# Another order of routing, projections and stack copies in the turns of a fused attention and mixture-of-experts kernel

## The chip, the core and the metric

One core of a Trainium2 chip runs the whole layer as one program. The metric is the device time of one execution in microseconds. Three runs of the kernel before gave 364.13, 364.21 and 365.44 us; the median is 364.21 us.

## What is computed

The input `x` is 4 batches of 512 tokens of width 256. It is normalized per token to `xn`, and the output is `x + attention(xn) + moe(xn)`, all in float32.

```
q = xn @ Wq (16 heads of 16); k = xn @ Wk, v = xn @ Wv (one head shared by all)
q, k = rope(q), rope(k)                      # first 8 of 16 dimensions
scores = q k^T / 4, allowed where 0 <= i - j < 64
attention = softmax(scores) v, heads joined, @ Wo + bo
logits = xn @ router_w; top 4 of logits + router_bias; gates = softmax(logits) of these, normalized to sum 1
routed = sum over the 4 of gate * (silu(xn wg_e) * (xn wu_e)) wd_e      # 64 experts, 256 x 64 x 256
shared = sum over 2 of (silu(xn swg) * (xn swu)) swd                    # hidden 256
```

## The kernel before, in words

The 2048 tokens are 16 tiles of 128. Each engine has a queue of its own, in an order written out by hand; semaphores tie them. In this kernel TensorE is `tensor(pe)`, ScalarE `scalar(act)`, VectorE `vector(dve)`, GpSimd `gpsimd(pool)` and the transfers' queue is `sync(sp)`. In the profile they are PE (its weight loads PEld), ACT, DVE, POOL and SP.

**Stages.** A first stage (to about 28 us) normalizes, transposes x, and makes keys, values and logits. Then comes "turn 0" and a loop of turns `T` = 1 to 15, one per tile of queries (28 to 146 us, turn T beginning where PE starts `maxima(T, 0)`). A tail (146 to 171 us) ends attention and starts the experts. Then 32 groups of four blocks of routed rows (to 277 us) and the shared expert with the sums follow.

**One turn.** Queries come from `project(T)` (L422: a matmul to bank 7 or bank 2; ACT's `copy_q`, L830, takes it to memory) and are rotated by POOL in pairs of tiles (`rotate`, L1517 to L1523: four pieces for a pair; `ROTATED_AT` says in which turn a pair starts, and a piece is done after each scatter of odd index). ACT `cast` (L854) and DVE `leave` (L1098) split them in bf16 parts, PE `stack` (L441) transposes them, ACT `stack` (L863) copies the result. PE `maxima(T, w)` (L463) makes scores by query, DVE `maxima` (L1104) reduces them, DVE `split` (L1113, L1115) cuts the maximum in two. PE `place` (L473) transposes it, DVE `place` (L1122) copies it out, and SP `place` (L1708) sends it by DMA to the rows that next turn's `scores` (L493) use. ACT `scores` (L871) is the exponential; `weigh` (L536) multiplies by values, DVE `output` (L1130) copies, `tokens` (L544), `attention` (L551, L877) and `project_out` (L561) follow. `stack_k` (L447) stands between the two `weigh` of a turn; it shares a bank with `place` and waits until DVE's `place` has read it. `project_out` and `project` share bank 7, each waiting for the reader of the other (`wide_free`).

**Routing.** DVE's `routing()` is a generator: `next(route)` does one piece, and `ROUTE`, `route_at` say how many pieces go before and after `place(T)`. Its seventh and eighth pieces make row numbers `slot_i` (L1231, semaphore `slots`); from then on POOL issues 64 scatters of xn rows (`scatter`, L1533), five in a turn up to T = 8, four later (`SCATTERED_AT`), each behind a wait for a step of PE in that turn. The last pieces make the gates, and from `expert_row` (L591, in turn 13) the experts' offsets `wslice`. SP loads the scattered rows (`load_block`, L1722) in turn 15, when all scatters have landed and the gates are ready.

**Late projections.** Tiles 0 to 6 are projected before turn 1, tile T + 6 in turn T (`late_tile`), between the last scores and `place(T)` on PE; ACT copies the query tile ahead of its second `stack` copy.

## Time and profile before

| what | us |
|---|---|
| median of three runs | 364.21 |
| profiled execution, its own time | 365.55 |
| its span | 364.2 |
| PE busy | 334.7 |
| DVE busy | 252.5 |
| POOL busy | 247.0 |
| ACT busy | 182.0 |

The span begins and ends with the first and last instruction; 1.35 us of the profiled execution lie outside it. Busy shares are means over all stages. For a change in the turns one reads the stretch of the turns: how long each turn takes, which engine was late at its end, and for whom it waited. The starts of the turns 2 to 15 (PE, line 463) are 47.87, 55.93, 63.54, 75.12, 82.95, 90.97, 98.75, 106.42, 113.45, 120.02, 126.49, 133.39, 140.22 and 146.11 us.

### The profile page before, as it was taken

Reading aid. Unit: us, or ns where it says so; the run is one execution under the profiler, and the core shown is the slowest. Engines: PE = TensorE matmul, PEld = TensorE weight load, DVE = VectorE, ACT = ScalarE, POOL = GpSimd, SP = SyncE. Lnnn points to the kernel's source line nnn. Section 1 sums busy time; section 2 is a strip of 40 time slices with the busy share of each in tenths; the row PEclk is TensorE's granted clock in tenths of the full one; section 3 lists DMA queues with packets and bytes.
Section 4 is the critical chain, followed back from the end, with each engine's and each line's share of the span. In section 5 each row is a group of like instructions: output and inputs, shape, how many; then the busy total and the mean of one; then the engine's idle time right before and its main releaser. Section 6 shows DMA issues by size and latency. Waiting matters only on the chain.

```text
span 364.2 us, 8589 instructions
## 1 busy us (share of the span) xinstructions
PE 334.7 (92%) x2711; PEld 248.2 (68%) x2711; DVE 252.5 (69%) x699; ACT 182.0 (50%) x344; POOL 247.0 (68%) x478
## 2 busy tenths in 40 slices
PE   6897879698999999999999999999999999999982
PEld 3795546456665665588999999999975456655572
DVE  4979888878899999555456545444476376667686
ACT  2696686857678787453655655555542111110100
POOL 6487378858778866224665667787884777777773
PEclk9998999989999999999999999999999999999999
DMA  8850245534586546899988855587975334444443
GB/s 247 228 157 1 61 162 158 166 131 158 159 249 199 153 162 173 251 240 265 319 270 264 267 181 169 187 246 254 331 254 161 105 115 130 131 127 121 134 140 115
DMA packets 73036, 66.83 MB, mean 183 GB/s; under 512 B 9053, under 2 KB 68701, under 8 KB 72993
## 3 DMA queue, kind: packets, MB, share of 16 engines
q1 hardware_dynamic: 66433, 49.30, 45.9%
q0 software_dynamic: 6144, 16.79, 14.7%
q8 instruction: 23, 0.38, 0.4%
q10 hardware_dynamic: 416, 0.20, 0.3%
q14 instruction: 20, 0.16, 0.2%
HBM read 36.79 MB, written 29.23 MB: 181 GB/s over the span
## 4 chain that ended last, share of the span: by engine, by line
PE 62%; DVE 12%; issue 8%; ACT 7%; POOL 6%; DMA 4%; SPq 1%; DVEq 0%; ACTq 0%; POOLq 0%
PE bank L669 16%; PE bank L608 15%; PE bank L694 9%; PE bank L628 7%; POOL xs_d L1533 5%; PE bank L643 5%; ACT xall L871 3%; PE bank L561 2%; ACT xall L863 2%; PE bank L536 2%; PE bank L422 2%; DMA spare<-xs_d 2%; DVE xall L1343 1%; DVE xall L1104 1%; DMA wall<-in_x 1%
## 5 line engine op out<-in xcount | busy, mean ns | idle before, releaser
L1533 POOL DMA_INDIRECT xs_d<-spare,slot_i x64 | 63.8, 998 | 30.5 <-issue 9.6
L1625 POOL DMA_INDIRECT wall<-y_d,y_row x64 | 62.8, 981 | 24.3 <-issue 18.9
L669 PE MATMUL bank<-xall,spare 128*128 x508 | 63.8, 278 | 0.0
L1297 DVE TENSOR_TENSOR spare<-bank,spare 64x512 f32<-64x512 f32 (+1 forms) x64 | 44.1, 690 | 28.2 <-ACT spare L912 27.3
L1560 POOL COPY spare<-wall 128x256 f32 x127 | 48.8, 406 | 20.7 <-PE bank L669 11.4
L669 PEld LDWEIGHTS bank<-xall,spare 128*128 128x128 f32 x508 | 59.4, 192 | 2.1
L608 PE MATMUL bank<-xnT,xall 128*128 128x512 f32 x128 | 57.3, 594 | 0.0
L925 ACT ACTIVATE spare<-bank 128x512 f32<-128x512 f32 (+1 forms) x62 | 33.6, 593 | 27.4 <-PE bank L694 21.1
L863 ACT ACTIVATE xall<-bank 98x1024 bf16<-98x1024 bf16 x32 | 32.8, 1025 | 17.6 <-PE bank L441 12.6
L608 PEld LDWEIGHTS bank<-xnT,xall 128*128 128x128 f32 x128 | 24.1, 190 | 25.2 <-issue 24.4
L888 ACT ACTIVATE xall<-bank 128x512 f32<-128x512 f32 x16 | 9.5, 597 | 59.6 <-PE bank L608 59.6
L871 ACT ACTIVATE xall<-bank 128x512 f32<-128x512 f32 x64 | 34.8, 604 | 4.4 <-PE bank L493 3.2
L1343 DVE SCALAR_TENSOR_TENSOR xall<-wall,gate,xall 128x256 f32<-128x256 f32 x64 | 31.1, 487 | 2.3
L912 ACT ACTIVATE spare<-bank 64x512 f32<-64x512 f32 (+1 forms) x32 | 18.8, 588 | 27.5 <-PE bank L669 27.5
L1165 DVE COPY xall<-bank 128x256 f32<-128x256 f32 x32 | 13.6, 424 | 25.2 <-PE bank L643 24.8
L1104 DVE TENSOR_REDUCE xall<-bank 128x4 f32<-128x316 f32 x64 | 28.0, 478 | 3.9 <-PE bank L463 3.5
L628 PEld LDWEIGHTS bank<-xall 128*128 128x128 f32 x128 | 24.2, 190 | 9.3 <-issue 5.3
L628 PE MATMUL bank<-xall 128*128 128x256 f32 x128 | 29.7, 380 | 1.0 <-DVE xall L1328 1.0
L854 ACT ACTIVATE xall<-xall 128x768 bf16<-128x768 f32 (+1 forms) x32 | 23.6, 739 | 11.1 <-POOL xall L1523 9.7
L1311 DVE SCALAR_TENSOR_TENSOR xall<-xall,bank 128x512 f32<-128x512 f32 x16 | 11.0, 687 | 21.4 <-ACT xall L888 21.3
L493 PE MATMUL bank<-xall,wdn 128*128 128x256 bf16 x120 | 20.9, 275 | 3.3 <-DMA xall<-xall 0.9
L441 PE MATMUL bank<-cb,xall 128*98 128x128 bf16 x256 | 20.7, 225 | 3.1 <-ACT xall L863 1.7
(174 smaller groups left out, 614.2 us busy)
## 6 DMA issues: line engine op xcount, KB each, us to landing
y_d<-spare SPq DMA_DIRECT2D x31, 512.0 KB, 3.7
wall<-in_wg SPq DMA_DIRECT2D x16, 256.0 KB, 3.6
wall<-in_wu SPq DMA_DIRECT2D x16, 256.0 KB, 4.2
wdn<-in_wd SPq DMA_DIRECT2D x16, 256.0 KB, 4.4
spare<-xs_d SPq DMA_DIRECT2D x32, 128.0 KB, 3.5
small<-xs_d SPq DMA_DIRECT2D x32, 128.0 KB, 3.4
wall<-in_x SPq DMA_DIRECT2D x4, 512.0 KB, 5.7
base_d<-spare SPq DMA_DIRECT2D x16, 128.0 KB, 3.9
```

The source lines that it names most:

```text
L608: ins = pe.matmul((gate_bank(i), up_bank(i))[half], wsh[:, c, half, ex, f0:f0 + P], xnT[:, c, g * GN:(g + 1) * GN], start=c == 0, stop=c = ...
L628: ins = pe.matmul(shared_bank(T), hs[T // GT % 2][:, k, t * P:(t + 1) * P], wshd[:, k, :], start=k == 0, stop=k == FC - 1)
L669: ins = pe.matmul(up_bank_of(G)[:, j * P:(j + 1) * P], wcur[i % NW][:, c * 2 * F:(c + 1) * 2 * F], x_half[c][:, bass.ds(o, P)], start=c == ...
L694: ins = pe.matmul(o[:, j * P:(j + 1) * P], hT[G % 2][rows64, j * P:(j + 1) * P], down_weights_of(G)[j][rows64, :], start=True, stop=True)
L863: act.activation(qS[0:SROWS + MROWS, T % NQ, :, 8 * i:8 * i + 8, :].rearrange("p u h q -> p h u q"), o[0:SROWS + MROWS].rearrange("p h (u ...
L871: act.activation(probs[n % 2][:, e * 512:(e + 1) * 512], bank[2 + e][:, :], ACT.Exp).then_inc(s["exp"], 1)
L925: act.activation(yb[G % 2][:, 0:n, half * P:(half + 1) * P], o[:, 0:n * P].rearrange("p (j d) -> p j d", d=P), ACT.Copy).then_inc(s["y_out ...
L1297: ins = dve.tensor_tensor(hT[G % 2][half, 0:n], up_bank_of(G)[F:P, 0:n], sg[0:F, 0:n], ALU.mult)
L1343: dve.scalar_tensor_tensor(a, yk[:, T, k, :], gate[:, T, k:k + 1], a, ALU.mult, ALU.add).then_inc(s["sum"], 1)
L1533: pool.indirect_dma_start(out=xs_d, out_offset=bass.IndirectOffsetOnAxis(ap=slot_i[:, T, k:k + 1], axis=0), in_=x_n[b][:, t, :], in_offset ...
L1560: pool.tensor_copy(wcur[i % NW].rearrange("p (c g f) -> p c g f", c=NC, g=2), wall[:, bass.ds(o, WE)].rearrange("p (g c f) -> p c g f", c= ...
L1625: pool.indirect_dma_start(out=yk[:, T, k, :], out_offset=None, in_=of, in_offset=bass.IndirectOffsetOnAxis(ap=y_row[:, T, k:k + 1], axis=0 ...
```

## The change

- **Turn 0**: PE projects tiles 4 to 7 there, not 4 to 6; `project(4)` moves ahead of `stack(1, 0)` and no longer does `kvr_read`; `maxima(1, 0)` of PE and DVE moves from turn 1 into turn 0 (DVE: ahead of the totals piece). POOL rotates tiles 6 and 7 before its first scatter.
- **Turns**: the late tile of turn T is T + 7, so turns 1 to 8 have one; PE does it behind `place(T)`. ACT copies its second stack ahead of the late query tile. DVE does its pieces of routing behind `place(T)` and `near(T + 1)`, ahead of `output(T - 1)`; two pieces in turns 9, 13 and 14, else one.
- **Routing**: the piece of the exponents' maximum comes ahead of the one for the expert of each block; the piece `y_row` stands by itself, later. `expert_row` is in turn 14.
- **POOL**: five scatters in every turn until they run out; the pair of tiles 8 and 9 begins in turn 2, then a pair every second turn to turn 8.

```diff
--- before.py
+++ after.py
@@ -323,11 +323,10 @@
 
     FIRST = 10
 
-    ROUTE = {8: (1, 1), 13: (0, 2)}
-    route_at = lambda T: ROUTE.get(T, (1, 0) if T < 8 else (0, 1))
-    EXPERT_ROW, EXPONENTS, BIAS_AT = 13, 4, 18
-    SCATTERED_AT = lambda T: (0, 1, 2, 3, 4) if T < 9 else (0, 1, 2, 3)
-    ROTATED_AT = {2: 6, 4: 8, 6: 10, 8: 12, 10: 14}
+    route_at = lambda T: 2 if T in (9, 13, 14) else 1
+    EXPERT_ROW, EXPONENTS, BIAS_AT = 14, 4, 18
+    SCATTERED_AT = lambda T: range(5)
+    ROTATED_AT = {2: 8, 4: 10, 6: 12, 8: 14}
     roped_with = lambda T: T + 1 if T < 2 else 2 + T // 2
 
     NORM = ((0,), (1,), (2,), (3,))
@@ -336,9 +335,9 @@
     ready = lambda T: (s["normed_act" if on_act(T) else "normed"], T // TPB * (TPB // 2) + T % (TPB // 2) + 1)
 
 
-    FIRST_LATE = 7
+    FIRST_LATE = 8
     late_tile = lambda T: (FIRST_LATE + T - 1,) if T + FIRST_LATE <= NT else ()
-    proj_bank = lambda T: bank[2 if T in (4, 6) else 7]
+    proj_bank = lambda T: bank[2 if T in (5, 7) else 7]
     rank_bank = lambda i: bank[(5, 3)[i]]
 
     KVR = P
@@ -411,13 +410,13 @@
                           ktok[:, 0:5, 0:SROWS], start=True, stop=True)
 
         def project(T):
-            if T == 4:
+            if T == 5:
                 kvr_read()
             if proj_bank(T) is bank[7]:
                 wide_free()
                 wide_reader.append((s["proj_q"], T + 1))
-            elif T == 6:
-                pe.wait_ge(s["proj_q"], 5)
+            elif T == 7:
+                pe.wait_ge(s["proj_q"], 6)
             for c in range(NC):
                 ins = pe.matmul(proj_bank(T)[:, 0:H * HD], xnT[:, c, T * P:(T + 1) * P], wproj[:, c, 0:H * HD],
                                 start=c == 0, stop=c == NC - 1)
@@ -483,7 +482,7 @@
             if w == 0 and e == 0:
                 pe.wait_ge(s[f"placed{T % 2}"], (T // 2 + 1) * MROWS * 16)
             if n == 0:
-                pe.wait_ge(s["proj_q"], 7)
+                pe.wait_ge(s["proj_q"], 8)
             elif n == 1:
                 pe.wait_ge(s["rank_read"], 2)
             if n >= 2:
@@ -714,20 +713,23 @@
         stack_k(1)
 
         maxima(0, 0)
+        project(4)
         stack(1, 0)
         maxima(0, 1)
-        project(4)
+        project(5)
         place(0)
         stack(1, 1)
-        project(5)
         project(6)
+        project(7)
+        maxima(1, 0)
         totals()
         for i in range(2):
             rank(i)
         stack_k(2)
 
         for T in range(1, NT):
-            maxima(T, 0)
+            if T > 1:
+                maxima(T, 0)
             if T + 1 < NT:
                 stack(T + 1, 0)
             if T > 1:
@@ -741,11 +743,11 @@
                 attention(T - 2)
             scores(T - 1, 1, 0)
             scores(T - 1, 1, 1)
-            for t in late_tile(T):
-                project(t)
             if T == EXPERT_ROW:
                 expert_row()
             place(T)
+            for t in late_tile(T):
+                project(t)
             if T < NT - 1:
                 weigh(T - 1, 0)
             if T + 2 < NT:
@@ -964,14 +966,15 @@
         copy_logits(0)
         copy_logits(1)
 
+        copy_q(4)
         cast(2, 0)
         stack(1, 0)
         cast(2, 1)
-        copy_q(4)
+        copy_q(5)
         stack(1, 1)
-        copy_q(5)
+        copy_q(6)
         cast(3, 0)
-        copy_q(6)
+        copy_q(7)
         act.wait_ge(s["c32"], 16)
         act.activation(unread[:, :], ident[:, 0:1], ACT.Exp)
 
@@ -988,10 +991,10 @@
                 attention(T - 2)
             scores(T - 1, 1, 0)
             scores(T - 1, 1, 1)
+            if T + 1 < NT:
+                stack(T + 1, 1)
             for t in late_tile(T):
                 copy_q(t)
-            if T + 1 < NT:
-                stack(T + 1, 1)
             if T == EXPONENTS:
                 exponents()
 
@@ -1231,6 +1234,11 @@
                 dve.tensor_scalar(slot_i[:, ts, :], gate_of[:, ts, :], ROUND, -ROUND, ALU.add, ALU.add).then_inc(s["slots"], 1)
                 yield
 
+            dve.wait_ge(s["logit"], 2)
+            chain(dve.tensor_reduce(emax, logit, AX.X, ALU.max))
+            yield
+            dve.tensor_tensor(expo, logit, emax.unsqueeze(2).to_broadcast([P, NT, E]), ALU.subtract).then_inc(s["shifted"], 1)
+            yield
             chain(dve.scalar_tensor_tensor(ends, ends, 1.0, k32["ends"], ALU.max, ALU.add))
             chain(dve.tensor_scalar(cmp, ends, k32["row"], None, ALU.is_le))
             chain(dve.tensor_reduce(blk_expert, cmp, AX.X, ALU.add))
@@ -1238,15 +1246,6 @@
             chain(dve.tensor_scalar(diag, ident, blk_expert, None, ALU.mult))
             dve.memset(onesf, 1.0).then_inc(s["diag"], 1)
             yield
-            dve.wait_ge(s["logit"], 2)
-            chain(dve.tensor_reduce(emax, logit, AX.X, ALU.max))
-            yield
-            dve.tensor_tensor(expo, logit, emax.unsqueeze(2).to_broadcast([P, NT, E]), ALU.subtract).then_inc(s["shifted"], 1)
-            dve.wait_ge(s["slots"], 2)
-            chain(dve.tensor_scalar(expert, pos8[:, :, 0:TOPK], -LIFT, None, ALU.add))
-            chain(dve.scalar_tensor_tensor(expert, slot_i[:, :, :], -CODE, expert, ALU.mult, ALU.add))
-            dve.scalar_tensor_tensor(y_row[:, :, :], expert, float(P), slot_i[:, :, :], ALU.mult, ALU.add).then_inc(s["rows"], 1)
-            yield
             dve.wait_ge(s["expo"], 1)
             chain(dve.tensor_reduce(esum, expo, AX.X, ALU.add))
             chain(dve.reciprocal(esum, esum))
@@ -1259,6 +1258,11 @@
                     ins = dve.max(gate8[:, t, :], lifted[:, t, :])
                 chain(ins)
                 yield
+            dve.wait_ge(s["slots"], 2)
+            chain(dve.tensor_scalar(expert, pos8[:, :, 0:TOPK], -LIFT, None, ALU.add))
+            chain(dve.scalar_tensor_tensor(expert, slot_i[:, :, :], -CODE, expert, ALU.mult, ALU.add))
+            dve.scalar_tensor_tensor(y_row[:, :, :], expert, float(P), slot_i[:, :, :], ALU.mult, ALU.add).then_inc(s["rows"], 1)
+            yield
             for i in range(4):
                 for t in range(4 * i, 4 * i + 4):
                     ins = dve.max_index(arg8[:, t, :], gate8[:, t, :], lifted[:, t, :])
@@ -1385,33 +1389,32 @@
         place(0)
         near(1)
         leave(2, 1)
+        maxima(1, 0)
+        next(route)
         next(route)
         next(route)
         for T in range(1, NT):
             if T + 1 < NT:
                 stack(T + 1)
-            maxima(T, 0)
             if T == 1:
                 next(route)
+            else:
+                maxima(T, 0)
             if T + 2 < NT:
                 leave(T + 2, 0)
             if T > 2:
                 add_x(T - 3)
             if T > 1:
                 tokens(T - 2)
-            if T == 1:
-                next(route)
             maxima(T, 1)
             split(T)
             if T + 2 < NT:
                 leave(T + 2, 1)
-            for _ in range(route_at(T)[0]):
-                next(route, None)
             place(T)
-            for _ in range(route_at(T)[1]):
-                next(route, None)
             if T + 1 < NT:
                 near(T + 1)
+            for _ in range(route_at(T)):
+                next(route, None)
             output(T - 1)
 
         turn(0)
@@ -1593,6 +1596,7 @@
         rotate_whole(2, 4)
         prepare_k(3)
         rotate_whole(4, 6)
+        rotate_whole(6, 8)
         slots, pieces = scatter(), iter(())
         for T in range(1, NT):
             if T in ROTATED_AT:
```

## Rows read from the trace of the kernel before

**Rows 1.** The page, its part on the chain that ended last: shares of the span

```profile
PE 62%; DVE 12%; issue 8%; ACT 7%; POOL 6%; DMA 4%; SPq 1%; DVEq 0%; ACTq 0%; POOLq 0%
```

**Rows 2.** Stretches: length, each engine's busy us, granted clock, DMA share, GB/s

```profile
47.87:106.42 58.55, 49.91 (x509) 33.35 (x505) 49.29 (x152) 42.11 (x71) 45.11 (x51) 0.97 0.55 173
106.42:146.11 39.69, 37.91 (x414) 25.00 (x413) 36.31 (x132) 31.00 (x52) 28.43 (x31) 1.00 0.58 170
63.54:75.12 11.58, 8.24 (x73) 5.19 (x72) 8.67 (x21) 7.58 (x12) 8.61 (x10) 0.89 0.47 150
106.42:113.45 7.03, 6.91 (x74) 4.61 (x73) 6.19 (x24) 5.06 (x9) 5.70 (x7) 1.00 0.59 173
120.02:126.49 6.47, 6.23 (x70) 4.00 (x69) 6.08 (x25) 4.73 (x9) 5.22 (x7) 1.00 0.63 188
140.22:146.11 5.89, 5.77 (x68) 3.88 (x67) 5.22 (x19) 4.26 (x7) 3.83 (x4) 1.00 0.75 195
146.11:171.40 25.29, 24.31 (x217) 18.71 (x215) 14.50 (x33) 12.36 (x26) 8.57 (x26) 1.00 1.03 249
```

**Rows 3.** Timeline of DVE around the place of turn 4

```profile
68.60 0.62 DVE L1115 TENSOR_TENSOR xall<-xall 128x16 bf16<-128x16 f32 x1
...
69.47 1.21 DVE L1244 TENSOR_TENSOR wdn<-wdn,small 128x1024 f32<-128x1024 f32 x1
...
71.82 0.20 DVE L1122 COPY xall<-bank 32x128 bf16<-32x128 bf16 x1
```

**Rows 4.** Waits from 30 to 160: in total, times, longest

```profile
PE bank L447 <- DVE xall L1122: 6.5, 8, 2.2
...
ACT xall L854 <- POOL xall L1523: 9.7, 6, 2.7
```

**Rows 5.** Timeline of PE, end of turn 11, a turn without a projection

```profile
123.97 0.23 PE L473 MATMUL bank<-cb,xall 128*32 128x128 bf16 x1
124.07 0.64 PE L536 MATMUL bank<-xall 128*32 128x256 f32 x8
...
124.95 0.64 PE L536 MATMUL bank<-xall 128*32 128x256 f32 x8
125.52 1.13 PE L561 MATMUL bank<-xall,spare 128*128 128x256 f32 x4
```

**Rows 6.** Timeline of PE, the projection of turn 9 and its place

```profile
110.17 1.03 PE L422 MATMUL bank<-xall,xnT 128*128 128x256 f32 x4
111.12 0.23 PE L473 MATMUL bank<-cb,xall 128*32 128x128 bf16 x1
```

**Rows 7.** Timeline of ACT, end of turn 11

```profile
123.62 1.10 ACT L871 ACTIVATE xall<-bank 128x512 f32<-128x512 f32 x2
124.58 1.06 ACT L863 ACTIVATE xall<-bank 98x1024 bf16<-98x1024 bf16 x1
```

**Rows 8.** Timeline of PE in turn 0

```profile
28.23 0.45 PE L463 MATMUL bank<-wdn,xall 128*128 128x79 bf16 x8 [0.22 <-DVE wdn L1090]
29.93 0.62 PE L441 MATMUL bank<-cb,xall 128*98 128x128 bf16 x8 [1.25 <-DVE wdn L1186]
```

**Rows 9.** Timeline of POOL: first scatter, a rotation piece, last scatter

```profile
44.77 1.19 POOL L1533 DMA_INDIRECT xs_d<-spare,slot_i  x1 [5.90 <-DVE slot_i L1231]
...
52.60 0.96 POOL L1533 DMA_INDIRECT xs_d<-spare,slot_i  x1 [0.30 <-issue]
53.59 0.75 POOL L1517 TENSOR_TENSOR xall<-xall,cf 128x256 f32<-128x256 f32 x1
54.50 1.01 POOL L1533 DMA_INDIRECT xs_d<-spare,slot_i  x1 [0.16 <-issue]
...
144.88 0.96 POOL L1533 DMA_INDIRECT xs_d<-spare,slot_i  x1 [0.31 <-issue]
```

**Rows 10.** Timeline of SyncE's queue: the first loads of scattered rows

```profile
148.14 1.81 SPq L1722 DMA_DIRECT2D spare<-xs_d  x4
```

**Rows 11.** Source line 1113: duration ns min/median/max

```profile
L1113 DVE CAST xall<-xall x16: 174/194/653, 32.6 to 149.1; 128x16 bf16<-128x16 f32 x16
```

## The prediction

> **What bounds the kernel now.** I read the views from the coarse to the fine. The page's chain puts 62% of the span on PE and 12% on DVE [rows 1]. Behind 171.4 us PE is nearly without a gap and the change touches nothing, so that stage only moves with its start. The question is how long the turns take. The stretches say it: turns 2 to 8 take 58.55 us, 8.4 each, with PE busy 49.91 of it; turns 9 to 14 take 39.69 us, 6.6 each, with PE busy 37.91 [rows 2]. Both sets do the same work per tile, but the early turns have a projection and pieces of routing ahead of the place of the maxima, and their POOL issues a scatter more. Turn 4 is the worst: 11.58 us at a mean granted clock of 0.89, against 6.47 us for turn 11 [rows 2].
>
> The DVE timeline says what the early turns wait for. In turn 4 the maximum was split at 68.60 + 0.62 = 69.2, and its copy-out stood behind routing until 71.82 [rows 3]. Behind this copy stands PE's key transpose (they share a bank) and then the second weighing, the output projection and the next turn: PE waited 6.5 us for it in 8 places [rows 4]. ACT's casts waited 9.7 us for POOL's rotations in 6 places [rows 4], which delays its stack copies and the scores behind them.
>
> **A turn after the change.** I build it from turn 11, which has no projection, no cast that waits, and its routing behind the place, as the new order has it. From one maxima to the next it takes 6.47 us [rows 2]. Its place is at 123.97, 3.95 us behind its start; then a weighing at 124.07, the key transpose, the second weighing at 124.95, and the output projection at 125.52 [rows 5]. A projection costs 111.12 - 110.17 = 0.95 us of PE [rows 6]. Put behind the place it shifts all that follows, except that the first weighing ended at 124.64 (the next starts at 124.95, held by DVE's place at 124.65): 0.15 us of wait goes under it. So a turn with a projection takes 6.47 + 0.95 - 0.15 = 7.27, say 7.3 us. Three covers carry this:
>
> - *Routing behind the place* (about 1.2 us a piece, as the one of turn 4 [rows 3]) is hidden behind PE's 0.95 + 0.6 + 0.2 + 0.6 = 2.3 us from the place to the second weighing's end, for which DVE's output waits anyway. If a piece were over 1.8 us, output and next turn's reductions would be late by the rest.
> - *ACT's query copy behind the stack copy.* New wait: the output projection shares bank 7 and waits for it; behind it on PE stand next turn's maxima. In turn 11 ACT starts its last exponentials at 123.62 and the stack copy at 124.58, which holds ACT for 0.95 us [rows 7]. The copy would follow at 125.5 and end at about 125.9. The output projection would start at 125.52 + 0.8 = 126.3. So it is hidden with 0.4 us to spare; without that cover it costs what ACT is late.
> - *The rotations* now run about two turns ahead of the cast that wants them, so the 9.7 us of ACT's waits go. What is late next is PE itself.
>
> Bounds of a turn: 7.03 us was measured for turn 9 [rows 2], which has its projection ahead of the place. From above I take 7.7, the 7.3 plus one blocked small DVE operation: the cast of the split takes 174 ns at best and 653 at worst [rows 11], 0.4 us more. Such long ones stand in turns in which POOL is busy, and POOL will be busy without a break. I take 7.3 since turn 11 has the new order of DVE.
>
> The Trainium skill, page "SBUF — State Buffer", section "Who interferes with whom", says that copies and casts of VectorE between rows of SBUF can want a port pair that GpSimd shares, and that the later of two then waits for all of the other's instruction. That speaks against a GpSimd that never pauses; the spread of the cast row agrees, and the upper bound of a turn stands for it.
>
> **The sum.**
>
> - Turn 0 and 1. The added projection is hidden. PE stood from the first maxima, 28.23 + 0.45 = 28.7, to 29.93 with 1.25 us of wait [rows 8]; project(4) needs only bank 7 and takes this gap. What follows in turn 0 keeps its times with tile T + 1 for T. In turn 1 the expected change is small: the first reduction is earlier, but a cast on ACT waits for DVE's leave, which now stands behind the slot piece. I take 0.15 us late, bounds 0.6 early and 1.0 late (a piece each way).
> - Turns 2 to 8: 7 x 7.3 = 51.1 against 58.55 [rows 2]: 7.45 us won.
> - Turns 9 to 14: 39.69 us before [rows 2]. Turn 9 has no projection now, 6.5. But DVE does two pieces (about 2.1 us) in it, in 13 (about 2.5) and in 14 (about 1.6), and with only 1.4 us of PE work behind the place to hide them. Turn 10 comes to 6.47 + 0.6 = 7.1, turns 11 to 13 to 6.5 each, turn 14 to 5.89 [rows 2] + 1.0 = 6.9. Together 40.0: 0.3 us lost.
> - Tail and all behind it keep their lengths. The first scattered rows are loaded relative to turn 15 (148.14 [rows 10], 2.0 us behind its start).
>
> Gain: 7.45 - 0.3 - 0.15 = 7.0 us. The span becomes 364.2 - 7.0 = 357.2, the profiled execution 365.55 - 7.0 = 358.55. The median run before, 364.21, lay 1.34 us under the profiled one and happens to equal its span; so I predict 357.2 us for the median.
>
> **POOL must keep up.** A scatter takes 0.96 + 0.30 us, and one with a rotation piece behind it 54.50 - 52.60 = 1.90, so a piece adds at most 0.64 [rows 9]. From the first scatter on it has 64 x 1.26 + 16 x 0.64 = 90.9 us of work (before, 20 pieces stood there; four now come earlier, in its 5.90 us of idle time). It starts at about 44.8 as before, since the slot piece ends within half a us of its old time. It ends at about 135.7, against 144.88 + 0.96 before [rows 9]. The loads would be wanted at about 148.14 - 7 = 141. So POOL isn't the end, by 5 us less the landing. One new wait: in turn 2 the rotation wants query tile 9, which that same turn projects. POOL comes there at 44.8 + 7 x 1.26 = 53.6 and the copy is ready at about 54.5: 0.9 us of stall. In turns 4, 6 and 8 POOL, at 7 to 7.6 us a turn, comes no earlier than the copies. The rotation of the last pair ends near 111, and its cast stands in turn 12, near 118.
>
> **Rivals.**
>
> 1. *The new order has its own waits* (chance 0.14). A turn with a projection takes 7.7 to 8.0 us, through bank 7's copy or through DVE operations blocked by POOL. For: the cover of the copy is 0.4 us only, the cast row reaches 653 ns. Against: ACT was ready early in turn 11. Seven turns cost 2.8 to 4.9 us more: 360 to 362.
> 2. *Transfers set the tail* (0.06). From 146.11 to 171.4 the DMA share is 1.03 [rows 2]; if transfers from the turns were still pushing there, a shorter loop would only bring the queue forward. For: that share. Against: in the turns it is 0.55 and 0.58, and the last scatters, which now reach up to the loads, will be over 5 us earlier. The gain would shrink to 0 to 2 us: 363.
> 3. *POOL becomes the end, slower* (0.06). The mechanism is the rotation's wait for the same turn's query copy. If POOL didn't lag, it would stand in four turns from its second scatter (about 2.5 us into the turn) to the copy (about 6 us): 3.5 us each, 14 us in all. The scatters would end at 135.7 + 14 = 149.7, and the loads would start at about 152 against 148.14: 4 us slower, 368. It decides from 10 us of stall. Against: POOL starts at turn 1 already 6 us behind PE and needs as long for a turn as PE.
>
> **How the numbers follow.** The forecast holds with 0.74: turns between 7.03 and 7.7 give 1.9 us less and 2.8 more, which with the bound of turn 0 and of turns 10 and 14 gives 354.5 to 360.3. To leave out no more than 2 in 10, the range reaches into the first rival: 354.5 to 361.0. This kernel's measurement can tell 0.5%, 1.8 us, from no change. Faster than 362.4 are the forecast and the first rival, 0.88, less a little for what I don't see: 0.87. Same: the second rival, 0.07. Slower: 0.06.
>
> **What would show it.** Right: turns 2 to 8 take about 7.3 us each and none stands out, clock 1.0 in turn 4; DVE's place within 0.4 us of its split; PE's wait for it and ACT's for rotations nearly gone; the last scatter at about 136. Turn 10 and 14 longer than before. Wrong: output projections that wait for ACT's query copy, scatters with gaps at the rotations, or a first load later than 2 us behind turn 15's start. The sum would be wrong if PE's work per turn grew longer with the DMA traffic packed closer, or if the clock fell in a place where it now holds.

## The result, and the profile after

The changed kernel takes 361.48 us at the median (360.64 to 363.08, six runs) against 364.93 for the one before in the same session (364.13 to 366.09): a ratio of 0.991 (0.988 to 0.994). Predicted were 357.2 us (354.5 to 361.0), a gain of 7.0; 3.45 us came. Medians are over all executions, while a ratio leaves out those over 1.5% above the fastest of the same kernel. Its profiled execution took 361.61 us with a span of 360.3, 3.9 us shorter than that of the profile before.

The page after, which answers to [rows 1]: the span, the busy times, the granted clock in 40 slices, and the shares of the chain that ended last.

```profile
span 360.3 us, 8591 instructions
PE 335.4 (93%) x2710; PEld 247.0 (69%) x2711; DVE 250.1 (69%) x699; ACT 180.6 (50%) x344; POOL 248.7 (69%) x478
PEclk9999969999999999999999999999999999999998
PE 72%; DVE 16%; ACT 5%; issue 4%; DMA 2%; DVEq 0%; ACTq 0%
```

PE's share of the chain rose from 62 to 72%, but one slice of the clock, from 45 to 54 us, reads 6. The stretches (length, then busy time and count of PE, PEld, DVE, ACT and POOL, granted clock, DMA share, GB/s) answer to [rows 2]; turn 2 now starts at 50.73, turn 9 at 104.06, turn 15 at 143.35.

```profile
50.73:104.06 53.33, 51.03 (x508) 32.95 (x505) 44.86 (x141) 41.04 (x71) 41.85 (x47) 1.00 0.57 172
104.06:143.35 39.29, 36.81 (x410) 24.43 (x409) 36.57 (x143) 30.68 (x51) 29.13 (x31) 1.00 0.61 184
66.34:73.81 7.47, 7.32 (x73) 4.66 (x72) 6.36 (x23) 6.53 (x11) 6.19 (x8) 1.00 0.55 174
81.19:88.57 7.38, 7.26 (x73) 4.67 (x72) 6.10 (x19) 5.68 (x10) 6.27 (x6) 1.00 0.49 160
...
46.00:50.73 4.73, 4.73 (x24) 1.84 (x23) 1.97 (x12) 2.94 (x5) 2.94 (x3) 0.50 0.51 161
```

The sum against the prediction's terms, from the starts of the turns in the two profiled executions:

| part | before | after | won | predicted |
|---|---|---|---|---|
| to turn 2 | 47.87 | 50.73 | -2.86 | -0.15 |
| turns 2 to 8 | 58.55 | 53.33 | 5.22 | 7.45 |
| turns 9 to 14 | 39.69 | 39.29 | 0.40 | -0.3 |
| from turn 15 on | 218.09 | 216.95 | 1.14 | 0 |

The seven turns took 7.72, 7.89, 7.47, 7.38, 7.38, 8.07 and 7.42 us. So two terms failed: the start, by 2.7 us, and a turn with a projection, 7.62 us in the mean where 7.3 stood. The 1.14 us of the last row, for which the forecast had 0, are no effect of the change, as the spread of that part below shows.

**The start.** These are rows of PE and ACT of the kernel before in turn 1 (start, length, instruction; in brackets the idle time before it and its releaser).

```profile
43.64 0.88 PE L493 MATMUL bank<-xall,wdn 128*128 128x256 bf16 x4 [0.64 <-ACT xall L871]
...
47.14 0.23 PE L447 MATMUL bank<-cb,xall 128*98 128x128 bf16 x1 [1.15 <-DVE xall L1122]
```
```profile
42.47 0.63 ACT L854 ACTIVATE xall<-xall 128x512 bf16<-128x512 f32 x1 [0.87 <-DVE xall L1098]
```

And ACT, DVE and PE of the changed kernel there:

```profile
44.01 0.63 ACT L856 ACTIVATE xall<-xall 128x512 bf16<-128x512 f32 x1 [2.61 <-DVE xall L1101]
44.55 1.06 ACT L873 ACTIVATE xall<-bank 128x512 f32<-128x512 f32 x2
```
```profile
43.47 0.18 DVE L1234 TENSOR_SCALAR slot_i<-wdn 128x32 int32<-128x32 f32 x1
43.56 0.42 DVE L1101 TENSOR_TENSOR xall<-xall 128x256 f32<-128x256 f32 x1
```
```profile
42.03 0.39 PE L492 MATMUL bank<-xall,wdn 128*128 128x256 bf16 x2 [1.18 <-DVE wdn L1223]
45.18 1.09 PE L492 MATMUL bank<-xall,wdn 128*128 128x256 bf16 x4 [2.31 <-ACT xall L873]
46.42 2.08 PE L421 MATMUL bank<-xall,xnT 128*128 128x256 f32 x4
48.43 1.08 PE L535 MATMUL bank<-xall 128*32 128x256 f32 x8
...
50.73 0.50 PE L462 MATMUL bank<-wdn,xall 128*128 128x79 bf16 x8
```

DVE's `leave` (43.56) now stands behind the slot piece; ACT's cast for it starts at 44.01, where before it started at 42.47, and the exponentials behind the cast at 44.55 instead of 43.01. PE stood 1.18 us for a rank piece and 2.31 us for these exponentials. So PE's second scores start 1.54 us later than before (45.18 against 43.64). Then the granted clock is 0.50, the lower level of 1.2 GHz, from 46 us on, and the projection takes 2.08 us instead of the 1.13 that it takes at full clock. The wait of 1.15 us for the copy-out, which the kernel before has here, is gone. POOL's added rotation (37.66 to 40.01 us) has a price too, for which the prediction had no term: beside it four small pieces of DVE's routing take 1.94 us instead of 1.34. That the rotation is the cause of it was not tested.

**A turn with a projection.** Turn 5, PE, in which nothing waits:

```profile
76.84 0.88 PE L492 MATMUL bank<-xall,wdn 128*128 128x256 bf16 x4
77.69 0.22 PE L472 MATMUL bank<-cb,xall 128*32 128x128 bf16 x1
77.84 1.13 PE L421 MATMUL bank<-xall,xnT 128*128 128x256 f32 x4
78.90 0.64 PE L535 MATMUL bank<-xall 128*32 128x256 f32 x8
...
81.19 0.45 PE L462 MATMUL bank<-wdn,xall 128*128 128x79 bf16 x8
```

From the second scores to the weighing it takes 78.90 - 76.84 = 2.06 us. From the place to the weighing are 1.21 us, where turn 11 of the kernel before has 0.10 [rows 5]: behind the place the projection costs 1.11 us, not 0.95. From one weighing to the other are 0.76 us (78.90 to 79.66), where turn 11 has 0.88.

**Turns 3 and 7** (7.89 and 8.07 us) are those in which small operations of DVE come out long, in turn 3 one `leave`, in turn 7 the cutting of the maximum:

```profile
59.60 1.01 DVE L1101 TENSOR_TENSOR xall<-xall 128x256 f32<-128x256 f32 x1
...
92.44 0.63 DVE L1118 TENSOR_TENSOR xall<-xall 128x16 bf16<-128x16 f32 x1
```
```profile
59.25 0.96 POOL L1536 DMA_INDIRECT xs_d<-spare,slot_i  x1 [0.30 <-issue]
...
92.30 0.73 POOL L1522 TENSOR_TENSOR xall<-xall,cf 128x256 f32<-128x256 f32 x1
```
```profile
61.62 0.44 PE L550 MATMUL bank<-cf,xall 128*128 128x128 f32 x2 [0.49 <-DVE xall L1143]
...
93.13 0.23 PE L472 MATMUL bank<-cb,xall 128*32 128x128 bf16 x1 [0.65 <-DVE xall L1118]
```

The `leave` of turn 3 started in the middle of a scatter of POOL and ended at 60.61, 0.40 us behind the scatter's end at 60.21; the same operation takes 0.41 to 0.43 us elsewhere. The subtraction of turn 7 (0.17 us in its short form) ended at 93.07, POOL's rotation beside it at 93.03. The Trainium skill, page "SBUF — State Buffer", section "Who interferes with whom", says that a VectorE instruction with two inputs in SBUF competes with a GpSimd instruction that reads SBUF, and that the one that issued first is not interrupted. The subtraction of turn 7, which started behind the rotation and ended with it, agrees. As a rule for scatters it does not come out here: of the 23 subtractions of this kind that start with or within a scatter's record, 21 take their short length (0.17 to 0.46 us), and only the one of turn 3 and one of turn 10 (114.48, 0.75 us) are long. Why these two, in the same place in `e5_changed` and `e14_changed` as well, is open. The casts of the maximum are more alike: in the kernel before, all seven that took over 0.25 us ended within 0.16 us of the end of a POOL instruction beside them. PE waited 0.49 us in turn 3 and 0.65 us in turn 7, nearly all that these turns take over 7.38.

### The profile page after: what moved, and what is told of

Read it like the earlier page. It is cut to its first block, busy times and chain, and to the rows that moved or that the text cites. A ratio compares the mean times of both kernels' runs of the same rounds, so it can differ in the third digit from the quotient of the medians.

```text
span 360.3 us, 8591 instructions
## 1 busy us (share of the span) xinstructions
PE 335.4 (93%) x2710; PEld 247.0 (69%) x2711; DVE 250.1 (69%) x699; ACT 180.6 (50%) x344; POOL 248.7 (69%) x478
## 4 chain that ended last, share of the span: by engine, by line
PE 72%; DVE 16%; ACT 5%; issue 4%; DMA 2%; DVEq 0%; ACTq 0%
PE bank L668 17%; PE bank L607 15%; PE bank L693 10%; PE bank L627 7%; PE bank L642 5%; PE bank L535 4%; PE bank L560 4%; PE bank L421 3%; DVE xall L1107 3%; ACT xall L873 2%; ACT xall L865 2%; DVE xall L1347 2%; DVE xall L1101 1%; DMA wall<-in_x 1%; PE bank L492 1%
## 5 line engine op out<-in xcount | busy, mean ns | idle before, releaser
L1536 POOL DMA_INDIRECT xs_d<-spare,slot_i x64 | 65.0, 1015 | 23.1 <-issue 13.2
L1563 POOL COPY spare<-wall 128x256 f32 x127 | 49.9, 415 | 22.9 <-issue 10.5
L535 PE MATMUL bank<-xall 128*32 128x256 f32 x256 | 21.3, 406 | 0.0
```

What stands on the lines that cost most here:

```text
L1536: pool.indirect_dma_start(out=xs_d, out_offset=bass.IndirectOffsetOnAxis(ap=slot_i[:, T, k:k + 1], axis=0), in_=x_n[b][:, t, :], in_offset ...
L1563: pool.tensor_copy(wcur[i % NW].rearrange("p (c g f) -> p c g f", c=NC, g=2), wall[:, bass.ds(o, WE)].rearrange("p (g c f) -> p c g f", c= ...
```

## The experiments

Each edit is against the changed kernel. Ratios are to the kernel before in the same session, with their 95% interval. Two of the five sessions fell on chips on which the kernel before takes 27 to 29 us more (391.8 and 392.9 us), and versions of the changed one 42 to 46 us more; they are told last.

**The changed kernel again, in two sessions.**

> The changed kernel itself, as the measure for the runs beside it, since the time differs from chip to chip. Expected: 0.991 of the kernel before (0.988 to 0.994), turn 2 starting at about 50.7 us with the clock of 38 us to turn 2 at about 0.74, turns 5 and 6 at 7.4 us, turn 15 starting near 143.4.

> The changed kernel. On a chip with 364 us before: 0.991 to 0.996 of before, turns 2 to 8 in 53.3, start of turn 2 between 49 and 51 us. On a chip with 392 us before: 1.02 to 1.03 of it. Its profile beside that of the kernel before says at which of the joint stops the 8 to 12 us come in.

363.09 us against 364.24, ratio 0.996 (0.993 to 0.999), and 361.62 against 363.64, 0.995 (0.992 to 0.998). So the gain is 1 to 3.5 us, depending on the session, and the length of turns 2 to 8 is stable: 53.40 and 53.36 us. Turn 2 started at 49.14 and 49.85.

**The kernel before, with a profile in the session of `e14_changed`.**

> The kernel before itself, for its profile beside the others of this call. Ratio 1.000 on either chip. On a chip where it takes about 364 us its turns 2 to 8 take 58.5 us and turns 9 to 14 39.7. On a chip where it takes about 392 us, theory S (all engines are held up together at certain places of the program, and a kernel loses by how many such places it has) expects joint stops of 1 to 6 us in this kernel too, some 27 us in all, but fewer or shorter in the turns than in the changed kernel; the rival (the stops are the same and the changed order bears them worse) expects the same stops and more waits of PE for DVE behind each.

363.75 us, ratio 1.000 (0.997 to 1.002), a span of 360.8. Its turns 2 to 8 took 56.93 us, not 58.55. Turn 4 is where they differ:

```profile
63.23:73.57 10.34, 6.99 (x73) 4.64 (x72) 8.58 (x21) 7.58 (x12) 7.75 (x10) 1.00 0.48 155
```

Turn 4 took 10.34 us at clock 1.00, against 11.58 at 0.89 in [rows 2]. The wait for the copy-out is the same 2.16 us. So 1.24 us of the 7.45 I forecast to be won were a low clock that this turn has in one execution and not in another. The part behind turn 15 took 216.6 us here and 218.1 in the profile before; over the profiled executions of all versions on the three chips like the first it runs from 216.4 to 219.6. The 1.14 us that the table shows there are no effect of the change.

**Where DVE's leave stands in turn 1.** `leave(3, 0)` ahead of the slot piece:

```diff
             if T == 1:
+                leave(T + 2, 0)
                 next(route)
             else:
                 maxima(T, 0)
-            if T + 2 < NT:
+            if 1 < T < NT - 2:
                 leave(T + 2, 0)
```

> The changed kernel with leave(3, 0) of VectorE ahead of the slot piece in turn 1, a second time (the first one's other stages were disturbed, but its turn 2 started at 47.50 at a clock of 1.00). Theory A: turn 2 starts at 47.5 to 48, the clock of the stretch is 1.0, everything behind it is 2.5 to 3 us earlier, ratio to the changed kernel 0.992. Rival: the gain is given back in turn 2 or by POOL, whose first scatter does not move; then turn 3 starts less than 1 us earlier than 58.45.

360.78 us, ratio 0.991 (0.987 to 0.995) beside 0.996 for the changed kernel in the session: 2.3 us less by the medians. PE's wait of 2.31 us shrank to 0.87. But in its profiled execution the clock was 0.50 from 46 us on even so, and turn 2 started at 49.80, later than the 49.14 of the changed one. The same code in another session (below) kept clock 1.00 and started turn 2 at 47.50. So the late cast is a cause, 1.4 us of PE's wait, but what it does to the start depends on the clock. Where in this profile the 2.3 us of the medians come from can't be told: its turns 2 to 8 take 53.65 us, and it is shorter than `e5_changed` only behind turn 15 (217.25 against 219.62 us), where versions differ anyway.

**The waits kept, the clock held.** 5 and 10 matmuls whose result nobody reads, in PE's two waits:

```diff
             elif n == 1:
+                keep_busy(5)
                 pe.wait_ge(s["rank_read"], 2)
+            elif n == 2:
+                keep_busy(10)
             if n >= 2:
                 pe.wait_ge(s["exp"], n - 1)
```

> The changed kernel, and in PE's waits of turn 1 (ahead of the rank piece's and ahead of the first scores') 5 and 10 matmuls into a free bank, whose result nobody reads, so that PE isn't idle there; every wait stays. Theory A (the low clock behind these gaps costs project, weighing and scores of turn 1 their double length): clock 1.00 from 38 us to turn 2, turn 2 starts at 48.5 instead of 49 to 51, the kernel 1 to 2 us faster than the changed one. The rival (the clock has little part in the late turn 2, ScalarE's late cast has all of it) expects less than 0.5 us of difference.

359.06 us, ratio 0.989 (0.985 to 0.993) beside 0.995 of the changed kernel: 2.6 us less by the medians. PE of this kernel (its lines are 7 further on behind L482, the added matmuls):

```profile
42.50 2.32 PE L482 MATMUL bank<-wdn,cb 128*128 128x512 bf16 x10
44.98 0.88 PE L499 MATMUL bank<-xall,wdn 128*128 128x256 bf16 x4 [0.16 <-ACT xall L880]
45.94 1.13 PE L421 MATMUL bank<-xall,xnT 128*128 128x256 f32 x4
47.01 0.64 PE L542 MATMUL bank<-xall 128*32 128x256 f32 x8
...
48.33 0.47 PE L462 MATMUL bank<-wdn,xall 128*128 128x79 bf16 x8
```

ACT's cast still waited 2.62 us, but the clock stayed at 1.00 through turn 1, the projection took 1.13 us, and turn 2 started at 48.33: 1.5 us ahead of the changed kernel's 49.85 on the same chip. PE's second scores started where they do without the fill (44.98 against 45.19), and from there to turn 2 it took 3.35 us. All profiles that have PE's order of this start bear it out, those of the slower chips too, whose slow stretches come later:

| start of the program | profiles | second scores to turn 2 | turn 2 starts | clock, 38 us to turn 2 |
|---|---|---|---|---|
| before: `before`, `e13` | 2 | 4.23 | 47.56, 47.87 | 1.00 |
| as changed, PE's order as changed: `after`, `e4`, `e5`, `e11`, `e14`, `e16` | 6 | 4.53 to 5.55 | 49.14 to 50.73 | 0.73 to 0.87 |
| with the fill: `e2`, `e9`, `e15` | 3 | 3.35, 3.36 | 48.33 to 48.55 | 1.00 |
| leave first: `e1` | 1 | 4.05 | 47.50 | 1.00 |
| leave first: `e6` | 1 | 6.03 | 49.80 | 0.77 |

So the low clock costs 1.2 to 2.2 us, and in the first profile 5.55 - 3.35 = 2.20 of the 2.86 us by which turn 2 was late. The other 0.66 us are the second scores, 1.54 us late, less 0.88 for a way to turn 2 that is shorter (3.35 us at full clock, without the wait for the copy-out, against 4.23). The rival, that the cast has it all, falls.

**The projection back ahead of the place, all else as changed.**

```diff
+            for t in late_tile(T):
+                project(t)
             if T == EXPERT_ROW:
                 expert_row()
             place(T)
-            for t in late_tile(T):
-                project(t)
```

> The changed kernel with only TensorE's order of late projection and place undone, a second time for an undisturbed look. Theory C (the order costs TensorE itself 0.35 us a turn, 7.38 against 7.03 in the same work): turns 4 to 8 take 7.0 to 7.1 us, turn 15 starts 2 to 2.5 us earlier, the whole 0.993 of the changed kernel. The prediction's view: place 0.95 us later delays what follows; turns 7.7 or more, whole slower by 2 us or more.

359.01 us, ratio 0.987 (0.983 to 0.990): 4.1 us less than the changed kernel by the medians. Turns 2 to 8 took 50.40 us instead of 53.40, turns 3 and 4 7.03 each. PE in turn 4:

```profile
67.33 0.88 PE L492 MATMUL bank<-xall,wdn 128*128 128x256 bf16 x4
68.05 1.03 PE L421 MATMUL bank<-xall,xnT 128*128 128x256 f32 x4
69.00 0.23 PE L472 MATMUL bank<-cb,xall 128*32 128x128 bf16 x1
69.02 0.65 PE L535 MATMUL bank<-xall 128*32 128x256 f32 x8
```

From the second scores to the weighing: 69.02 - 67.33 = 1.69 us, for the same instructions that take 2.06 in the order place, projection. The 0.37 us come in three parts: with the place between scores and projection, the place starts 0.13 us later behind the scores than the projection does here, 0.13 more pass from the place to what follows it, and the projection takes 0.11 more. That is the 0.35 us between 7.38 and 7.03, and the changed kernel has it in every turn, 2.45 of the 3.0 us. The rest goes with the two long turns: turn 3 took 7.03 and turn 7 7.22 us here, and no turn but the second (7.68 us) over 7.23.

**Routing back ahead of the place, the projection behind it.**

```diff
+            for _ in range(route_at(T) if 1 < T < 9 else 0):
+                next(route, None)
             place(T)
             if T + 1 < NT:
                 near(T + 1)
-            for _ in range(route_at(T)):
+            for _ in range(0 if 1 < T < 9 else route_at(T)):
                 next(route, None)
```

> The changed kernel with DVE's piece of routing in turns 2 to 8 ahead of place(T), as before the change; all else as changed. The prediction's theory (the copy-out of the maximum, late behind the piece, was what made these turns 8.4 us) expects PE's waits for it back, about 1 us in each turn with a piece over 1 us and 3 us in turn 4: 4 to 7 us slower than the changed kernel. The rival (the bank it holds is wanted late enough since projection and weighing stand behind the place, and the gain came from POOL's rotations) expects at most 2 us slower.

362.58 us, ratio 0.998 (0.995 to 1.001) beside 0.995: 1.0 us more by the medians. Turns 2 to 8 took 54.10 us against 53.36. The prediction's cause wanted 4 to 7 us more. PE has no wait for the copy-out in these turns. So what stands behind the place on PE, projection and weighing, covers nearly a whole piece of routing.

**Both orders back, then ScalarE's too.** `e17` has both edits above. `e18` adds:

```diff
+            for t in late_tile(T):
+                copy_q(t)
             if T + 1 < NT:
                 stack(T + 1, 1)
-            for t in late_tile(T):
-                copy_q(t)
```

> The changed kernel with two of its orders back to those of before in turns 2 to 8: PE's projection ahead of place(T), and DVE's piece of routing ahead of it. Turn 0, the later late tile, the earlier rotations, the row piece by itself and later, and ScalarE's stack copy ahead of the queries stay as changed. Each of the two orders alone was seen: projection ahead made the turns 7.1 us, routing ahead alone 7.7. Theory I (the projection behind the place is the cover that hides a piece of routing: with neither, PE's key transpose waits for a copy-out that stands behind the piece) expects waits of 0.7 to 1.2 us at the key transpose in the four or five turns whose piece is over 1 us: turns 2 to 8 in 52 to 53.5 us, the kernel about 1.0 of the changed one. The rival (nothing waits for the copy-out, and only the long piece of turn 4 of before did harm) expects turns of 7.1 us, 50 in all: 2.5 to 3.5 us faster than the changed kernel. On a chip where the kernel before takes 392 us only the waits can be compared.

> As the last one, and ScalarE's query copy ahead of its second stack copy as before the change. Of the change there stay turn 0, the rotations two turns earlier and the row piece by itself. Theory T (the changed kernel's gain is that of the early rotations and of the row piece that no longer stands ahead of a place in turn 4) expects turns 2 to 8 in 52 to 54 us, as e17, the kernel within 1 us of the changed one and 0.990 to 0.996 of the one before. The rival (ScalarE's order carries the gain, by stack copies that come 0.4 us earlier) expects 0.4 us more in every turn, 55 to 56.5 us for turns 2 to 8, and the kernel as slow as the one before.

361.13 us, ratio 0.990 (0.988 to 0.993), and 360.52 us, ratio 0.991 (0.988 to 0.994). Turns 2 to 8 took 52.33 and 52.37 us. In turn 5 of `e17` DVE's copy-out stood behind a piece again, and PE waited:

```profile
76.61 1.21 DVE L1250 TENSOR_REDUCE small<-wdn 128x16 f32<-128x1024 f32 x1
...
78.15 0.21 DVE L1125 COPY xall<-bank 32x128 bf16<-32x128 bf16 x1
```
```profile
78.51 0.23 PE L446 MATMUL bank<-cb,xall 128*98 128x128 bf16 x1 [0.58 <-DVE xall L1125]
```

PE's waits for the copy-out in turns 2 to 8 (in total, times, longest), first `e13_before`, then `e17`, then `e18`:

```profile
PE bank L447 <- DVE xall L1122: 5.8, 7, 2.2
```
```profile
PE bank L446 <- DVE xall L1125: 2.3, 5, 0.6
```
```profile
PE bank L446 <- DVE xall L1125: 1.7, 4, 0.6
```

Against `e7`, in another session, 52.33 - 50.40 = 1.9 us is what routing behind the place is worth when the projection stands ahead. The kernel with all three orders of before is as fast as the changed one: what it keeps of the change is turn 0, the rotations two turns earlier, the scatters and pieces of routing as the change has them, and with these the row piece out of turn 4. Its waits of ACT's casts for rotations are gone in turns 2 to 8, where `e13_before` has 5.1 us of them, and its turn 4 takes 7.51 us. Which of these parts brings how much of the 4.6 us between 56.93 and 52.37 was not separated. ScalarE's order made no difference that these runs can tell: 52.37 against 52.33.

**What was learned, together.** Leave first, projection ahead of the place, routing behind it, and the double pieces in turns 7, 8 and 14 (`route_at = lambda T: 2 if T in (7, 8, 14) else 1`):

> The changed kernel with leave(3, 0) first, the late projection ahead of place, and the double pieces of routing in turns 7, 8 and 14 in place of 9, 13 and 14 (so that turn 13 has 0.9 us of routing, not 2.5). If the causes are right they add: 3.0 for turn 1, 2.4 for the order, 0.8 for turn 14, together 6 us under the changed kernel, 355.5 us, ratio to the kernel before 0.975. If they overlap (TensorE waits for something else once it is faster), 358 to 360.

357.24 us, ratio 0.982 (0.978 to 0.986): 7.0 us under the kernel before, and 5.85 under the changed one, beside it. Turn 2 starts at 46.48 with clock 1.00, turns 2 to 8 take 51.99 (the longest are turn 4, 7.72, and turn 8, 7.83), turns 9 to 14 38.75. The parts were expected to add to 6 us under the changed kernel, and by the medians they nearly do. By the profiles the start brings 2.7 us, turns 2 to 8 1.4 where 2.4 were expected, turns 9 to 14 0.6; the rest of the 7.5 us between the two spans lies behind turn 15.

**On the two slower chips.** The first four were meant to tell apart the start (leave, fill), the projection's place and the routing's place; the edits are those above.

> The changed kernel with one edit: in turn 1 VectorE does leave(3, 0) ahead of the slot piece of routing, not behind it. Theory A (the start is where the gain went): ScalarE's cast(3, 1) no longer sits 2.6 us, the exponentials of tile 0 start near 43.0 instead of 44.55, TensorE's 2.3 us gap shrinks under 1 us, the clock of the stretch from 38 us to turn 2 comes back from 0.74 to above 0.9, turn 2 starts at 48.0 to 49 instead of 50.73, and the whole is 2 to 3 us faster than the changed kernel (359 us). Rival B (the clock falls for other reasons, such as the wait of 1.2 us for the rank pieces): turn 2 starts at 50 or later, gain under 1 us.

> The changed kernel with matmuls added that nobody reads (5 ahead of the second and 10 ahead of the third scores matmul pair of tile 0, into bank 7), so that TensorE isn't idle in its two gaps of turn 1 while every wait stays. It measures what the low clock of turn 1 costs by itself. Theory A: the gaps stay as long, but the clock stays near 1.0, the projection of turn 1 takes 1.1 us instead of 2.08 and the weighings 0.6 instead of 1.08; turn 2 starts near 48.9, 1.5 to 2 us earlier than 50.73, and the whole is 1.5 to 2 us faster than the changed kernel. Rival: the waits alone set the start of turn 2; then it stays at 50.5 or later and the time at 361.5.

> The changed kernel with TensorE's order in the turns undone: the late projection ahead of place again, all else as changed. From turns 5 and 6 of the changed kernel (7.38 us each, TensorE without a gap) against turn 9 of the kernel before (7.03 us, same work, projection first) theory C says that the order itself costs TensorE 0.35 us a turn: turns 4 to 8 then take 7.03 us, and the whole is about 2.4 us faster than the changed kernel. The prediction's view (place first frees the next turn) says the opposite: turns grow by what place is late, 0.3 to 0.9 us each, 2 to 6 us slower.

> The changed kernel with the pieces of routing of turns 2 to 8 ahead of VectorE's place again, all else as changed. The prediction's cover (pieces hide behind the projection and the two weighings) says that without it the key transpose waits in each such turn about 1.2 us less the 0.95 us of projection that now stands behind place: turns of 7.7 us and more, the whole 2 to 4 us slower than the changed kernel, with the wait of the key transpose back. Rival: TensorE's own work hides it here too, and the time stays at 361.5 within 0.7 us.

Against 391.77 us they took 405.16 (ratio 1.028, 1.021 to 1.036), 403.75 (1.034, 1.027 to 1.041), 403.61 (1.026, 1.018 to 1.033) and 406.98 us (1.042, 1.034 to 1.050). In the third session, against 392.91 us:

> The changed kernel with the unread matmuls in TensorE's two gaps of turn 1 (5 and 10 of them), every wait kept, a second time for the time of the whole. Theory A in its refined form (of the late start of turn 2, the larger part is the low clock that follows the gaps): the clock of 38 us to turn 2 is 1.00 in this and turn 2 starts near 48.4 as before, 1 to 2 us earlier than in the changed kernel, and the whole is 1 to 2 us faster than its 0.991 to 0.996 of the kernel before, so 0.989. Rival: filling changes nothing that can be measured.

> The kernel with the three edits (leave first, projection ahead of place, pieces spread; 357.24 us, 0.982) with the same unread matmuls added. If its runs differ by the clock of turn 1 (0.990 to 0.996 over the span, 355.0 to 358.9 us), the slow ones go: about 355.5 us and a spread under 2 us. If filling delays TensorE's own work it is slower by up to 1 us.

> The changed kernel with the routing pieces of turns 2 to 8 ahead of VectorE's place, a second time. The first look fell on a disturbed stage. The cover of the prediction says: the key transpose waits again in these turns (1.2 us of piece less the 1.06 us of projection that stands there), turns of 7.5 to 8.2 us in place of 7.38, whole 1 to 4 us slower than the changed kernel. Rival: the projection behind place hides the pieces as well, and the time is that of the changed kernel; then the gain of the new place of routing is nil as long as the projection stands behind place.

> The kernel with the three edits, and VectorE's order at the start of turn 1 as in the kernel before: the first reductions of tile 1 behind the two pieces of totals and the first rank piece, not ahead of them. Expected: TensorE's wait of 1.18 us for the rank piece shrinks to 0.3 to 0.5 us, so that its gaps are shorter and the clock holds more often: 356 us, 1 us under the three edits. Rival: the reductions only change places with the pieces and the second reduction is as late as before, then 357.2 within 0.7.

404.52 us (1.030, 1.024 to 1.036), 399.11 (1.012, 1.007 to 1.017), 404.25 (1.029, 1.025 to 1.033) and 405.52 (1.020, 1.013 to 1.027). `e10` is the code of `e8` with the fill, `e12` that of `e8` with DVE's first maxima and rank piece of turn 1 where they stood before the change. All these expectations were made for a chip like the first and were missed by their whole time. What can be used is the stretch up to turn 2, ahead of the slow stretches: in the first of these sessions turn 2 started at 47.50 us with the leave first, at 48.46 with the fill, and at 49.39 and 49.60 in the two that have neither; in the other at 48.55 with the fill and 49.97 without (`e11`), at 47.54 in `e10` and 47.89 in `e12`. In `e12` PE's wait of 1.18 us gave way to one of 1.71 us for the first maxima, and the clock was 0.83 even so. The edits of `e8` pay here too: `e10` took 5.4 us less than `e9`, which has the fill alone. Behind turn 2, the same program on two chips, 50 to 146 us, first `e9_fill`, then `e15_fill`:

```profile
50.00:146.00 96.00, 78.04 (x724) 50.31 (x724) 64.43 (x220) 58.90 (x98) 61.44 (x68) 0.89 0.48 146
```
```profile
50.00:146.00 96.00, 91.18 (x939) 58.42 (x937) 83.95 (x288) 73.24 (x127) 70.51 (x76) 1.00 0.60 182
```

## Why the prediction was right and wrong

The measured 361.48 us lie above the stated 361.0. The term that failed most is the start of turn 2, and in it the clock, for which the sum had nothing: without its 2.20 us this time would be 359.3 us, an estimate from the trace, and the kernel with the fill took 359.06. The second is the 7.45 us of turns 2 to 8. Two things made the miss smaller: turns 9 to 14 came 0.7 us better than said, and the 1.14 us behind turn 15 are luck. The time falls among the 360 to 362 us of the first rival, but not by its mechanism alone: its seven turns were to cost 2.8 to 4.9 us more, and cost 2.2.

**The start of turn 2: wrong, and the largest miss.** The step said that the change in turn 1 is small, 0.15 us late with bounds 0.6 early and 1.0 late, because "a piece each way" was all that moved. It named the cast that waits for the leave behind the slot piece, and didn't follow the wait to its end: cast, exponentials behind the cast on ACT, PE's second scores (2.31 us of wait). At full clock these waits and the new order make turn 2 0.66 us late, within the bounds. What lay outside them was the clock, 2.20 of the 2.86 us. Clock 1.00 stood in that stretch before, and with PE idle twice it didn't hold. The prediction's last sentence, "if the clock fell in a place where it now holds", is the case that came; it should have been a rival with a price: turn 1's PE work from 46 us on at half speed.

**A turn with a projection: right in kind, 0.3 us too short.** The floor of the new order is 7.38 us, not 7.27. The credit for a wait under the projection came nearly as said, 0.12 us of 0.15. What was too small is the projection's price: 1.11 us behind the place, where 0.95 stood, read from a turn in which it stands ahead of it. And the bound from below, 7.03 us of turn 9, belonged to the old order of PE; the edit costs 0.35 us a turn in itself, which adding a projection's length to turn 11 couldn't show. The blocked small operation of the upper bound came in turn 3 and turn 7 and was put too low: 0.4 us forecast, and turns of 7.89 and 8.07 us where 7.7 was the bound. In turn 7 two long cuts of the maximum (0.50 and 0.63 us) held PE's place for 0.65 us. As a mean the bound held: 7.62.

**The first rival** (own waits of the new order) came in in one half only. DVE's long small operations, beside POOL's, made turns 3 and 7 long; bank 7's copy did not: in turn 6 the query copy ended at 87.09 and the output projection started at 87.60 without a wait, half a us of cover where 0.4 was forecast.

**Turns 2 to 8 of the kernel before.** 7.45 us were to be won from 58.55, of which 1.24 are turn 4's low clock in that one execution. Against `e13_before` the changed turns of the same session win 56.93 - 53.36 = 3.6 us, so this term was mis-sized by more than the table says, which fits the 1 to 2 us by which the medians differ in the later sessions.

**Routing behind the place: the smaller part of the cause.** The [rows 3] show a copy-out behind routing and [rows 4] PE's wait of 6.5 us for it; I took the order as the remedy. By `e16` the order alone is worth 0.7 us of turns 2 to 8 and 1.0 of the whole, and by `e18` the kernel without any of the three orders has the same time. With the projection ahead it is worth 1.9 us (`e17` against `e7`). Of PE's 5.8 us of waits for the copy-out in `e13_before`, `e18` has only 1.7 left, though its routing stands ahead of the place as before. The longest of them, 2.16 us, was made in turn 4 by the piece with the row numbers, which has moved out of it, and what ACT waited for were rotations that came late.

**Turns 9 to 14: 39.29 us, 40.0 forecast.** Turn 9 took 6.52 as said; turn 10 took 6.62, not 7.1, so its cover held; turn 14 took 7.08, 6.9 forecast, where PE waited 0.91 us for an output behind 2.5 us of routing.

**POOL: not the end, but 5 us later than reckoned.** It reached the rotation of turn 2 at 54.6 where 53.6 was forecast, and the query copy came at 57.05, not 54.5, with the late turn 1: 2.5 us of stall where 0.9 was forecast. The last scatter ended at 140.08 + 0.96 = 141.0, not at 135.7, a sum that left out this stall and 3.8 us in which scatters waited for steps of PE. POOL's next work began 10.5 us later, at 151.52, so the third rival didn't come. The first load of scattered rows was issued at 146.15, 2.8 us behind the start of turn 15, which the prediction had named as a sign of being wrong; the last scatter had ended 5 us before, and the part behind turn 15 was no longer for it. Nor did the second rival come: the DMA share of that stage is 0.99, and it was no longer than before. Of ACT's waits for rotations, 9.7 us in [rows 4], one of 1.2 us ahead of turn 1 is left, and in the turns two of 0.2 for DVE.

**What stays open.** Why PE's order costs 0.35 us a turn wasn't separated: in the one order the short bf16 place stands between scores and projection, in the other between projection and weighing. How turn 0, the earlier rotations and the moved pieces of routing share what `e18` keeps is open too. What the clock does in turn 1 isn't fully told by PE's waits, since `e6` lost it with shorter ones, and `e1`, the same code, didn't. And why all versions of the changed kernel that ran on the slower chips are 1 to 4% slower than the one before there is unknown, for there is no profile of the one before from those chips.

## What to carry to other kernels

When an edit moves work ahead of a wait early in a program, follow the wait through every engine to PE and then ask whether PE's new idle time takes its clock: here waits and order made turn 2 0.66 us late and the clock another 2.20. Price a new order of two matmul groups by its own floor, from start to start, not by adding a group's length to a turn that lacks it. And before crediting an order with a wait seen in the trace, ask which single piece made the wait: here a kernel that moved that one piece and started the supply two turns earlier, with the three orders left as before, took the same time as the whole reordering. The best version (0.982) kept routing behind the place, which `e7` and `e17` together show to pay, and took the projection back ahead of it.

## What the runs showed of the hardware

The granted clock of one program differs between its executions: turn 1's last stretch had 0.50 (from 46 us) in the first profile and 0.67 (46 to 50 us) in `e14_changed`, turn 4 of the kernel before 0.89 and 1.00. With waits of PE of 0.63 or 0.99, 0.64 and 1.15 us in this stretch it held in both profiles of the kernel before. It fell after PE had stood for 1.18 and 2.31 us, in all six profiles with that start, and once after 1.18, 0.87 and 0.53 us; with nearly the same waits (1.18, 0.87 and 0.62) it held in `e1_leave_first` (1.00 from 38 to 47.5 us). The Trainium skill, page "TensorE: Matmul & The Clock Gate", part "The HAM clock gate", says that the default is the throttled state and activity lifts it, and that where a program falls in the monitoring differs from run to run; the profiles of one code, `e6` with 0.50 and `e1` with 1.00, agree with that.

Two of the chips ran the kernel before 7 to 8% slower and the versions of the changed one 11 to 13%, with stretches in which all engines get less done at once: in the same 96 us, `e9_fill` got 78.0 us of PE and 64.4 of DVE done, `e15_fill` 91.2 and 84.0, with fewer bytes moved (146 against 182 GB/s), so a higher load on the transfers is not what is seen. The order that wins 1.8% on the one kind of chip (`e8`) lost 1.2% on the other (`e10`, with the fill).
